# Two multiplications in GpSimd's rounding of attention weights, and one VectorE product left out

## The chip, the cores and the metric

The kernel runs on one core of one Trainium2 chip. The metric is the device time of one execution in microseconds; the median over runs is compared. The profile is taken from one execution by the hardware profiler.

## The reference

Four transformer layers follow one another on an activation x of 2 x 512 tokens by 128 features, with a context of 2 x 77 tokens. Layer 0 attends from the ten best tokens, layer 1 has single-head attention, layer 2 has 16 heads with rotary positions, and layer 3 is quantised to 8 bits. The change touches only layer 3's self-attention. Cut to what matters:

```python
def _fq(x, delta, zp, n_bits):
    xi = _round_ste(x / delta) + zp
    xq = jnp.clip(xi, 0.0, 2.0 ** n_bits - 1.0)
    return (xq - zp) * delta

# 16 heads of 8 features, 2 x 512 tokens; dq = dk = dv = 0.02, dw = 1 / 255
sim = jnp.einsum('bhid,bhjd->bhij', _fq(q, dq, 128.0, 8), _fq(k, dk, 128.0, 8)) * SCALE
attn = jax.nn.softmax(sim, axis=-1)
out = jnp.einsum('bhij,bhjd->bhid', _fq(attn, dw, 0.0, 8), _fq(v, dv, 128.0, 8))
```

So an attention weight becomes the integer nearest to exp(s - max) / (sum x dw), at most 255.

## The kernel before, in words

Each engine has its own hand-written list of instructions, and semaphores order them against each other. There is no planner: the order of each list is as it stands in the code. The self-attention of layer 3 is worked off in 64 pairs. A pair n is two heads (j = 0, 1) of one block of 128 query tokens against all 512 keys, so two tiles of 128 x 512 values. Its way through the engines:

- TensorE, `int_scores(n)` (L865): two matmuls of the integer queries and keys write the scores into two PSUM banks. Three pairs of banks take turns.
- VectorE, `maxima(n)` (L1430): the negative maximum of every row of both tiles, written to `stats[:, 0]`.
- GpSimd, `shift(n)` (L441): multiplies the two maxima of a row by the score's scale, giving `stats[:, 1]`.
- ScalarE (L1048): two activations compute exp(scale x score + shift) into one of six slots of `e_ring` and add up each row's sum in `stats[:, 3]`.
- VectorE, `recips(m)`, once for two pairs (four sums a row): L1436 multiplies the sums by the step dw (`sc(DW1)`), in place, and waits for itself; L1437 takes the reciprocal into `stats[:, 2]`.
- GpSimd, `rounded(n)` (L450), two instructions a pair: multiplies each row of 512 exponentials by its reciprocal, adds the constant 0.0 and writes int16, which rounds. The output goes to one of four slots of `t_rows`.
- The SP queue (L334): a DMA transposes the pair's 128 x 1024 integers. It waits for both roundings of the pair, and for the key conversion of the pair four before.
- VectorE, `keys(n)` (L1443): the transposed integers, cut at 255, become bf16.
- TensorE, `int_outputs(n)` (L882): the product with the integer values, accumulated in PSUM.

The orders are skewed. GpSimd's list is shift(n), then rounded(n - 3); VectorE's is maxima(n), then recips every second n (for pairs n - 3 and n - 2), then keys(n - 6); TensorE's is int_scores(n), then int_outputs(n - 7). ScalarE has one pair after the other. `rounded(n)` waits for the reciprocal of its two pairs and for the transpose of pair n - 4.

`sders` is a small tile written once by VectorE near the start of the kernel: its columns 0 to 7 are the reciprocals of the eight quantisation steps, so `sders[:, DW1]` is 1 / dw, one value on all 128 partitions. L1138, L1416 and the shift L441 read other columns of it.

On GpSimd, far ahead of this stage, two kinds of instruction alternate four times each: L385 multiplies a tile of 154 elements a row by a column and adds the constant 0.0, and L387 multiplies the same tile by a column and adds a second column. L397, in every layer norm, adds a constant to 4 elements a row.

Of the kernel before, what the change touches and what calls it, by code (L numbers as in the profile page):

```python
# [10 lines left out]
ALU = mybir.AluOpType  # L11
# [47 lines left out]
DQ1, DK1, DV1, DW1, DQ2, DK2, DV2, DW2, SCORE_B = range(9)  # L59
# [20 lines left out]
def spare_row(v):  # L80
    return BAND - 1 - DH * v
# [23 lines left out]
def build(nc, ins, out, stop=99):  # L105
    ctx = ExitStack()
    with ctx:
        def sb(name, shape, dt=F32):
            return ctx.enter_context(nc.sbuf_tensor(name, shape, dt))
# [27 lines left out]
        def S(name):  # L137
            name = shared.get(name, (name, 0))[0]
            if name not in sems:
                sems[name] = ctx.enter_context(nc.semaphore(name.replace(".", "_")))  # L140
            return sems[name]
# [58 lines left out]
        stats = sb("stats", [P, 8, 16])  # L200
        q_stack = sb("q_stack", [P, U * N], BF16)
        k_stack = sb("k_stack", [P, U * N], BF16)
        sders = sb("sders", [P, 16])
# [53 lines left out]
        def sc(k):  # L257
            return scalars[:, k:k + 1]
# [7 lines left out]
        def turned(n):  # L266

            return S(f"L3.turned{n % TURNING}"), 16 * (n // TURNING + 1)
# [76 lines left out]
        def _(pool):  # L345
# [90 lines left out]
            def shift_pairs():  # L436

                def shift(n):
                    c = 2 * (n % 8)
                    pool.wait_ge(S("ints.nm"), n + 1)  # L440
                    pool.tensor_scalar(stats[:, 1, c:c + 2], stats[:, 0, c:c + 2], sders[:, 8:9], None, ALU.mult  # L441
                                       ).then_inc(S("ints.m"), 1)

                def rounded(n):
                    pool.wait_ge(S("ints.recip"), n // 2 + 1)
                    if n >= TURNING:
                        pool.wait_ge(*turned(n - TURNING))
                    for j in range(2):
                        c = 2 * (n % 8) + j
                        pool.tensor_scalar(t_rows[n % TURNING][:, j, :], e_ring[n % len(e_ring)][:, j, :],  # L450
                                          stats[:, 2, c:c + 1], 0.0, ALU.mult, ALU.add).then_inc(S("ints.rounded"), 1)

                for n in range(PAIRS + ROUND_BEHIND):
                    if n < PAIRS:
                        shift(n)
                    if n >= ROUND_BEHIND:
                        rounded(n - ROUND_BEHIND)
# [612 lines left out]
        def _(dve):  # L1070
            own = [0]

            def then(ins):

                own[0] += 1
                ins.then_inc(S("dve.own"), 1)
                dve.wait_ge(S("dve.own"), own[0])
# [233 lines left out]
            s = ps[0:80, 7, 0:4 * M].rearrange("p (n m) -> p n m", m=M)  # L1311
# [45 lines left out]
            if stop >= 2:  # L1357
# [31 lines left out]
                for i in range(T):  # L1389
                    dve.wait_ge(S("heads.sc"), count("L2.ca", "sc") + i + 1)  # L1390
                    at = i * V * P + spare_row(0)
                    c = P + spare_row(1) - spare_row(0)
                    nm = neg_max[:, at:at + V * c].rearrange("p (v c) -> p v c", c=c)[:, :, 0:3 * BAND + 1:BAND]
                    s = ps[:, 4 * (i % 2):4 * (i % 2) + 4, 0:V * M].rearrange("p j (v m) -> p v j m", v=V)
# [8 lines left out]
            if stop >= 3:  # L1403
# [29 lines left out]
                def recips(m):  # L1433
                    s, r = (stats[:, k, 4 * (m % 4):4 * (m % 4) + 4] for k in (3, 2))
                    dve.wait_ge(S("ints.exp"), 4 * (m + 1))
                    then(dve.tensor_scalar(s, s, sc(DW1), None, ALU.mult))  # L1436
                    dve.reciprocal(r, s).then_inc(S("ints.recip"), 1)  # L1437

                def keys(n):
# [6 lines left out]
                for n in range(PAIRS + KEYS_BEHIND):  # L1446
                    if n < PAIRS:
                        maxima(n)
                    m = n - ROUND_BEHIND
                    if 0 <= m < PAIRS and m % 2 == 0:  # L1450
                        recips(m // 2)
                    if n >= KEYS_BEHIND:
                        keys(n - KEYS_BEHIND)
# [9 lines left out]
                for n in range(B * FC):  # L1463
                    k, c = divmod(n, FC)
# [32 lines left out]
```

## Time and profile before

| | us |
|---|---|
| median of 3 runs | 682.29 |
| lowest, highest run | 680.37, 683.24 |
| profiled execution | 681.98 |
| its span, first to last instruction | 680.3 |
| GpSimd busy in the span | 202.8 |
| VectorE busy in the span | 413.2 |
| stretch of the 64 pairs, roughly | 403 to 532 |

Busy time is the time in which an engine has an instruction in execution. A wait for a semaphore is not part of it, but a wait that happens inside an instruction is. The chain of waits is followed back from the last instruction, at each step to what released it or to the instruction before it on its engine. "issue" in it is time in which the engine waited for nothing that the profile shows.

### The profile page before, as it was taken

To read this page: it belongs to the slowest core of one execution; us is meant where nothing else is said; L and a number is where in the kernel's file an instruction comes from. 1 tells how busy PE (TensorE), PEld (TensorE's weight loads), DVE (VectorE), ACT (ScalarE), POOL (GpSimd) and SP (SyncE) were. 2 spreads that over 40 slices of the span, in tenths; PEclk is the share of its full clock that TensorE was granted. 3 is DMA by queue.
4 is the path that set the end of the run, shared out by engine and by line. 5 is a ranking of instruction groups with operands and counts; after the bars stand their busy time and mean duration, and the time that the engine had idled before them with its cause. 6 is when DMAs were issued, how large, how long until landed. Compare 5 with 4: busy or idle time off the path is not lost.

```text
span 680.3 us, 8234 instructions
## 1 busy us (share of the span) xinstructions
PE 443.0 (65%) x2905; PEld 243.9 (36%) x2905; DVE 413.2 (61%) x854; ACT 248.0 (36%) x481; POOL 202.8 (30%) x354
## 2 busy tenths in 40 slices
PE   6578459266767998758986635556655435545577
PEld 3445245133334333425243511222222313334435
DVE  3625470758896111258333489899998478888543
ACT  2014123021001666310624119888886112313131
POOL 3220222500000334240002209899989200000020
PEclk9559658688898999865977875555555665555569
DMA  9100000000000000000000006887887200000001
GB/s 281 50 0 1 1 0 1 0 0 1 1 1 1 1 1 1 1 1 0 1 1 0 1 0 121 133 148 139 142 142 144 27 0 0 1 0 1 0 1 31
DMA packets 75804, 23.43 MB, mean 34 GB/s; under 512 B 67894, under 2 KB 74996, under 8 KB 75764
## 3 DMA queue, kind: packets, MB, share of 16 engines
q1 hardware_dynamic: 75763, 22.91, 17.5%
q8 instruction: 23, 0.38, 0.2%
q14 instruction: 18, 0.14, 0.1%
HBM read 5.60 MB, written 0.52 MB: 9 GB/s over the span
## 4 chain that ended last, share of the span: by engine, by line
PE 38%; DVE 30%; POOL 19%; issue 8%; ACT 3%; DMA 1%; ACTq 0%; DVEq 0%; POOLq 0%
POOL k_stack L450 12%; DVE k_stack L1380 6%; PE ps L631 3%; DVE xh L1093 3%; PE ps L563 3%; POOL stats L441 3%; PE ps L486 3%; PE ps L587 3%; PE ps L671 3%; PE ps L617 3%; PE ps L556 2%; PE ps L482 2%; POOL rstd L399 2%; DVE cr_max L1186 2%; PE ps L578 2%
## 5 line engine op out<-in xcount | busy, mean ns | idle before, releaser
L397 POOL TENSOR_SCALAR rstd<-mv 128x4 f32<-128x4 f32 x18 | 4.1, 227 | 268.6 <-DVE mv L1088 268.5
L1430 DVE TENSOR_REDUCE stats<-ps 128x2 f32<-128x1024 f32 x64 | 77.4, 1213 | 1.8 <-PE ps L865 1.8
L960 ACT ACTIVATE e_buf<-ps 128x1024 f32<-128x1024 f32 (+4 forms) x56 | 39.7, 771 | 106.0 <-PE ps L617 105.3
L1048 ACT ACTIVATE e_buf<-ps,stats,sders 128x512 f32<-128x512 f32 x88 | 67.6, 775 | 25.7 <-POOL stats L441 25.6
L882 PE MATMUL ps<-k_stack,q_stack 128*32 128x128 bf16 x512 | 39.2, 308 | 46.8 <-DVE k_stack L1443 46.7
L450 POOL TENSOR_SCALAR k_stack<-e_buf,stats 128x512 int16<-128x512 f32 x88 | 62.4, 721 | 1.4
L671 PE MATMUL ps<-ident,e_buf 128*77 128x128 f32 x128 | 33.3, 430 | 34.9 <-ACT e_buf L969 34.9
L1380 DVE TENSOR_REDUCE k_stack<-ps 128x4 f32<-128x512 f32 (+3 forms) x32 | 46.1, 1488 | 9.5 <-PE ps L590 9.5
L882 PEld LDWEIGHTS ps<-k_stack,q_stack 128*32 128x32 bf16 x512 | 22.3, 129 | 77.0 <-DVE k_stack L1443 76.5
L347 POOL TENSOR_SCALAR_AFFINE_SELECT e_buf<-e_buf 128x256 f32<-128x256 f32 x44 | 17.6, 407 | 107.4 <-ACT e_buf L960 106.4
L865 PE MATMUL ps<-q_stack 32*128 32x512 bf16 x128 | 38.0, 603 | 14.0 <-DVE q_stack L1424 7.4
L482 PE MATMUL ps<-ident,xh 128*128 128x128 f32 x72 | 19.3, 432 | 41.7 <-DVE xh L1093 41.7
L587 PE MATMUL ps<-q_stack,qT 32*128 32x128 f32 (+3 forms) x256 | 29.7, 537 | 21.7 <-DVE k_stack L1380 11.7
L1107 DVE TENSOR_TENSOR x<-ps,x 128x512 f32<-128x512 f32 x14 | 9.7, 692 | 51.8 <-PE ps L563 38.1
L671 PEld LDWEIGHTS ps<-ident,e_buf 128*77 128x77 f32 x128 | 25.1, 243 | 39.9 <-ACT e_buf L969 39.9
L1443 DVE TENSOR_SCALAR k_stack<-k_stack 128x1024 bf16<-128x1024 int16 x64 | 28.8, 449 | 11.8 <-DMA k_stack<-k_stack 11.6
L919 ACT ACTIVATE xT<-ps,cols 128x512 f32<-128x512 f32 x12 | 9.3, 777 | 72.7 <-PE ps L482 72.7
L617 PE MATMUL ps<-k_stack,q_stack 32*128 32x512 f32 (+3 forms) x256 | 33.8, 477 | 0.7 <-ACT e_buf L960 0.6
L1159 DVE COPY o_sb<-ps 128x512 f32<-128x512 f32 x16 | 11.0, 687 | 36.1 <-PE ps L631 36.1
L1048 ACT ACTIVATE t_buf<-ps,stats,sders 128x512 f32<-128x512 f32 x40 | 30.8, 777 | 3.1 <-POOL stats L441 3.1
L1093 DVE TENSOR_SCALAR xh<-x,mv,rstd 128x128 f32<-128x128 f32 x72 | 28.5, 458 | 4.0 <-POOL rstd L399 4.0
L482 PEld LDWEIGHTS ps<-ident,xh 128*128 128x128 f32 x72 | 13.3, 219 | 45.7 <-DVE xh L1093 45.2
(250 smaller groups left out, 953.2 us busy)
## 6 DMA issues: line engine op xcount, KB each, us to landing
wsq<-in_squares SPq DMA_DIRECT2D x3, 384.0 KB, 5.0
k_stack<-k_stack SPq DMA_TRANSPOSE x64, 3.1
spread<-in_spread SPq DMA_DIRECT2D x1, 896.0 KB, 6.8
x<-in_x SPq DMA_DIRECT2D x1, 512.0 KB, 4.4
l_w<-in_L_xattn_W_ff SPq DMA_DIRECT2D x2, 256.0 KB, 7.2
l_w<-in_L_xattn_fc_w SPq DMA_DIRECT2D x2, 256.0 KB, 7.8
l_w<-in_L_xattn_ff_w SPq DMA_DIRECT2D x1, 512.0 KB, 8.8
out<-x SPq DMA_DIRECT2D x2, 256.0 KB, 2.3
```

What stands on the lines that cost most here:

```text
L450: pool.tensor_scalar(t_rows[n % TURNING][:, j, :], e_ring[n % len(e_ring)][:, j, :], stats[:, 2, c:c + 1], 0.0, ALU.mult, ALU.add).then_in ...
L482: mm = pe.transpose(ps[:, k, t * P:(t + 1) * P], src[:, k * QB + t, :], ident[:, :])
L587: mm = pe.matmul(ps[:, 4 * (i % 2) + j, 0:n], qT[r, at:at + P], keys(r), start=True, stop=not causal)
L617: mm = pe.matmul(ps[0:rows, 2 * slot + j % 2, 0:N - kb * P], keys(b, v, r, kb), q_shift[r, b, v, kb * P:N], start=True, stop=True)
L671: mm = pe.transpose(ps[0:M, 3 + c % 2, j * P:(j + 1) * P], e_buf[:, i % 2, h * M:(h + 1) * M], ident[:, :])
L865: mm = pe.matmul(ps[:, 2 * (n % 3) + j % 2, :], tile(q_int, b * QB + qb)[r, :], k_band[r, v, b * N:(b + 1) * N], start=True, stop=True)
L882: mm = pe.matmul(ps[BAND * band:BAND * (band + 1), 7, qb * P:(qb + 1) * P], v_band[:, kb, b, V * band + v, :], t_keys[n % len(t_keys)][:, ...
L960: act.activation(e_ring[n % len(e_ring)][0:rows, :, 0:N - kb * P], ps[0:rows, 2 * (n % 3):2 * (n % 3) + 2, 0:N - kb * P], ACT.Exp).then_in ...
L1048: act.activation(e_ring[n % len(e_ring)][:, j, :], ps[:, 2 * (n % 3) + j, :], ACT.Exp, bias=stats[:, 1, c:c + 1], scale=sders[:, 8:9], acc ...
L1093: ins = dve.tensor_scalar(xh[:, t, :], x[:, t, :], mv[:, t, 0:1], rstd[:, t:t + 1], ALU.subtract, ALU.mult)
L1380: dve.tensor_reduce(nm, ps[:, 4 * (i % 2):4 * (i % 2) + 4, 0:(qb + 1) * P], AX, ALU.max, negate=True).then_inc(S("heads.max"), 1)
L1430: dve.tensor_reduce(stats[:, 0, c:c + 2], ps[:, 2 * (n % 3):2 * (n % 3) + 2, :], AX, ALU.max, negate=True).then_inc(S("ints.nm"), 1)
```

## The change

The rounding's second scalar operand is the column 1 / dw in place of the constant 0.0, and its second operation a multiplication in place of an addition. The product of sum and dw on VectorE, with the wait for it, is left out; the reciprocal is taken of the sum itself. The integer that results is that of exp x (1 / sum) x (1 / dw).

```diff
@@ -448,7 +448,8 @@
                     for j in range(2):
                         c = 2 * (n % 8) + j
                         pool.tensor_scalar(t_rows[n % TURNING][:, j, :], e_ring[n % len(e_ring)][:, j, :],
-                                          stats[:, 2, c:c + 1], 0.0, ALU.mult, ALU.add).then_inc(S("ints.rounded"), 1)
+                                          stats[:, 2, c:c + 1], sders[:, DW1:DW1 + 1], ALU.mult, ALU.mult
+                                           ).then_inc(S("ints.rounded"), 1)
 
                 for n in range(PAIRS + ROUND_BEHIND):
                     if n < PAIRS:
@@ -1433,7 +1434,6 @@
                 def recips(m):
                     s, r = (stats[:, k, 4 * (m % 4):4 * (m % 4) + 4] for k in (3, 2))
                     dve.wait_ge(S("ints.exp"), 4 * (m + 1))
-                    then(dve.tensor_scalar(s, s, sc(DW1), None, ALU.mult))
                     dve.reciprocal(r, s).then_inc(S("ints.recip"), 1)
 
                 def keys(n):
```

## Rows read from the trace of the kernel before

**Rows 1.** The page's first part: busy us (share of the span) and instructions.
```profile
PE 443.0 (65%) x2905; PEld 243.9 (36%) x2905; DVE 413.2 (61%) x854; ACT 248.0 (36%) x481; POOL 202.8 (30%) x354
```

**Rows 2.** Windows, stretch 409 to 527 us: length, busy us by engine, clock, DMA.
```profile
409.00:527.00 118.00, 69.95 (x614) 27.42 (x614) 108.06 (x184) 99.21 (x248) 110.17 (x189) 0.50 0.80 139
```

**Rows 3.** Chain of waits, 409 to 527 us: shares by line.
```profile
by line: POOL k_stack L450 68.7%; POOL stats L441 17.8%; issue 13.5%; POOLq L447 0.1%
```

**Rows 4.** Timeline of GpSimd: start us, duration us, instruction, count.
```profile
417.48 0.53 POOL L441 TENSOR_SCALAR stats<-stats,sders 128x2 f32<-128x2 f32 x1
...
424.68 0.43 POOL L441 TENSOR_SCALAR stats<-stats,sders 128x2 f32<-128x2 f32 x1
425.08 1.35 POOL L450 TENSOR_SCALAR k_stack<-e_buf,stats 128x512 int16<-128x512 f32 x2
426.42 0.28 POOL L441 TENSOR_SCALAR stats<-stats,sders 128x2 f32<-128x2 f32 x1
426.76 1.46 POOL L450 TENSOR_SCALAR k_stack<-t_buf,stats 128x512 int16<-128x512 f32 x2
428.23 0.42 POOL L441 TENSOR_SCALAR stats<-stats,sders 128x2 f32<-128x2 f32 x1
```

**Rows 5.** Timeline of VectorE, same round.
```profile
426.01 0.45 DVE L1436 TENSOR_SCALAR stats<-stats,scalars 128x4 f32<-128x4 f32 x1
426.49 0.18 DVE L1437 RECIPROCAL stats<-stats 128x4 f32<-128x4 f32 x1
426.59 0.41 DVE L1443 TENSOR_SCALAR k_stack<-k_stack 128x1024 bf16<-128x1024 int16 x1
...
428.05 0.45 DVE L1443 TENSOR_SCALAR k_stack<-k_stack 128x1024 bf16<-128x1024 int16 x1
```

**Rows 6.** Timeline of GpSimd at the start of the stage.
```profile
410.51 0.29 POOL L441 TENSOR_SCALAR stats<-stats,sders 128x2 f32<-128x2 f32 x1
410.77 1.36 POOL L450 TENSOR_SCALAR k_stack<-e_buf,stats 128x512 int16<-128x512 f32 x2
412.10 0.29 POOL L441 TENSOR_SCALAR stats<-stats,sders 128x2 f32<-128x2 f32 x1
412.46 1.36 POOL L450 TENSOR_SCALAR k_stack<-e_buf,stats 128x512 int16<-128x512 f32 x2
```

**Rows 7.** Lines L385, L387: ns min/median/max, then three of their rows in the timeline.
```profile
L385 POOL TENSOR_SCALAR km<-kc,band_mask x4: 396/408/426, 29.4 to 32.0; 128x154 f32<-128x154 f32 x4
L387 POOL TENSOR_SCALAR k<-kc,band_mask,band_one x4: 465/484/503, 29.8 to 32.4; 128x154 f32<-128x154 f32 x4
...
29.84 0.47 POOL L387 TENSOR_SCALAR k<-kc,band_mask,band_one 128x154 f32<-128x154 f32 x1
30.29 0.40 POOL L385 TENSOR_SCALAR km<-kc,band_mask 128x154 f32<-128x154 f32 x1
30.67 0.50 POOL L387 TENSOR_SCALAR k<-kc,band_mask,band_one 128x154 f32<-128x154 f32 x1
```

**Rows 8.** Single lines over the whole kernel: ns min/median/max, first and last start.
```profile
L450 POOL TENSOR_SCALAR k_stack<-e_buf,stats x88: 685/687/964, 409.2 to 526.2; 128x512 int16<-128x512 f32 x88
L441 POOL TENSOR_SCALAR stats<-stats,sders x64: 282/290/528, 404.8 to 520.7; 128x2 f32<-128x2 f32 x64
L1436 DVE TENSOR_SCALAR stats<-stats,scalars x32: 214/452/653, 408.6 to 522.8; 128x4 f32<-128x4 f32 x32
L397 POOL TENSOR_SCALAR rstd<-mv x18: 224/228/241, 72.3 to 648.6; 128x4 f32<-128x4 f32 x18
```

**Rows 9.** Late transposes: landing times, waits of 409 to 527 us, two timeline rows.
```profile
DMA to landing us min/median/max: 3.0/3.1/5.3
...
POOL stats L441 <- DVE stats L1430: 7.2, 6, 1.8
...
435.36 0.43 DVE L1443 TENSOR_SCALAR k_stack<-k_stack 128x1024 bf16<-128x1024 int16 x1 [1.60 <-DMA k_stack<-k_stack]
437.02 0.39 POOL L441 TENSOR_SCALAR stats<-stats,sders 128x2 f32<-128x2 f32 x1 [1.80 <-DVE stats L1430]
```

## The prediction

> **What bounds the kernel now.** I read the page's busy line first and the table of windows second. Over the whole kernel no engine stands out, but in the stretch of the change, 409 to 527 us, GpSimd is busy 110.2 of 118.0 us and VectorE 108.1, with ScalarE at 99.2 and the DMA engines at 0.80 [rows 1, 2]. Two engines are nearly full, so the share alone does not say which one a saving must be made on. The chain of waits for that stretch does: 68.7% is the rounding of L450, 17.8% the shift of L441, the rest issue, and no VectorE line is in it [rows 3]. The timeline of GpSimd shows why: in one round of two pairs, 424.68 to 428.23 us, that is 3.55 us, its instructions touch each other, two roundings, a shift, two roundings, a shift, with one visible gap of 0.06 us ahead of the rounding at 426.76 [rows 4].
>
> VectorE looks as full in its own timeline, but part of that is waiting inside an instruction. The product of L1436 has 4 elements and takes 0.45 us here, from 426.01 to 426.46, and over the stage it runs from 214 to 653 ns, median 452 [rows 5, 8]. It ends as the rounding on GpSimd ends (425.08 + 1.35 = 426.43) [rows 4, 5]. So about 0.24 of its 0.45 us is VectorE standing behind GpSimd, and VectorE has that much to spare in a round.
>
> The opposite also shows. The shift takes 0.43 and 0.42 us where VectorE's key conversion L1443 runs beside it (428.05 to 428.50), and 0.28 where none does; two roundings take 1.46 beside the L1443 of 426.59, and 1.35 without [rows 4, 5]. Undisturbed spacing stands at the stage's start: two roundings 1.33 us (410.77 to 412.10), a shift 0.26 (410.51 to 410.77) [rows 6]. A round of GpSimd without collisions is thus 2 x (1.33 + 0.26) = 3.18 us; the measured 3.55 holds 0.37 more: two collisions of about 0.14 each with L1443, and 0.09 of waiting for the reciprocal.
>
> By the Trainium skill (SBUF — State Buffer, Who interferes with whom) GpSimd and a VectorE instruction in a 2-port mode hold one port pair exclusively, so that "the other fully blocks". The trace agrees in kind (0.45 against 0.214 us for L1436). What that rule alone would promise from dropping a port user is not found on GpSimd's side: the shift that follows L1436 takes its least, 0.28.
>
> **The change part by part.** The stage has 64 pairs, 128 roundings and 32 calls of recips.
>
> First, the rounding's second scalar becomes a column in place of the constant 0.0: 128 instructions, all on the chain. The kernel has the same contrast elsewhere on GpSimd. L385 multiplies 154 elements by a column and adds the constant 0.0; L387 multiplies by a column and adds a column, same size, alternating with it. Their least durations are 396 and 465 ns (69 apart), their medians 408 and 484 (76 apart), and their starts give 0.45 us from L387 to the next and 0.38 from L385 to the next (29.84, 30.29, 30.67) [rows 7]. Is this price per instruction or per element? An instruction with one column costs 0.26 us of spacing at 2 elements and 1.33 / 2 = 0.665 at 512, so 0.79 ns an element [rows 6]; that line gives 0.38 at 154 elements, which is what L385 shows. So the one-column form has a fixed part of about 0.26 us. L397, with 4 elements and no column at all, has a median of 228 ns against 290 for the shift L441 with one column [rows 8], so the first column costs about 60 ns at a size where elements cost nothing. The second, at 69, is nearest to that: I take it as fixed. 128 x 0.069 = +8.8 us. Bounds: 0 below (if the read of the second column hides behind the 512 elements), and above it grows with the elements, 0.076 x 512 / 154 = 0.25 us each, +32 us. Below nothing is excluded: the new form has no fewer operands or operations. The second operation also turns from an add into a multiplication, for which no GpSimd row exists; as both are one operation an element I take no difference, and the same +32 covers a slower multiplication.
>
> By the Trainium skill (Advanced Engine Details and Errata, GPSIMD Details) a per-partition read on GpSimd has about 50 ns of latency; by that, an estimate, the sum's term would be 128 x 0.05 = 6.4 us in place of 8.8, and the sum 684.2 us. The least durations of L385 and L387, 69 ns apart, are taken instead.
>
> Second, VectorE's L1436 goes: 32 instructions of 0.45 us and the wait behind them; from its start to that of the reciprocal it is 426.01 to 426.49 = 0.48 us [rows 5]. None of this lies on the chain except at one point: the reciprocal ends at 426.49 + 0.18 = 426.67 and the rounding that needs it starts at 426.76, 0.34 us after its shift's start, where an undisturbed one starts 0.26 after [rows 4 to 6]. With the reciprocal 0.48 earlier GpSimd never waits for it. The wait was 0.08 to 0.10 us in some 30 rounds: -2.7 us. Bounds: 0 and 32 x 0.10 = -3.2.
>
> Third, transposes that land late. Their landing takes 3.1 us, at most 5.3 [rows 9]. Where one is late, VectorE's L1443 waits (1.60 us at 435.36), its maximum L1430 of the next pair is late, and GpSimd's shift stands idle: 1.80 us at 437.02. In the stretch there are six such idle times with 7.2 us together; the first, 1.46 us, is the start of the stage, so 5.7 us are five late landings [rows 9]. L1443 of pair n - 6 needs a rounding three pairs behind the shift, so slower pairs give the landing more time: with roundings 0.14 us longer a pair and the wait and jitter taken off, about 0.1 x 3 = 0.3 us of each. 5 x 0.3 = -1.5 us. Bounds: 0, and all 5.7 us if VectorE, 0.48 us a round lighter, gets far enough ahead; it is held back by the same transposes, so I stay near the low end.
>
> Fourth, collisions. L1443 stays, 64 times, and now arrives about 0.4 us earlier in every second pair. Each costs GpSimd 0.14 us today. The dearest row is the shift of 0.53 us at 417.48, 0.25 above its least [rows 4]; the cheapest is 0.10. L1436 itself cost GpSimd nothing. I take no change: 0. Bounds: 64 x (0.25 - 0.14) = +7 us and, if they all vanish, 64 x 0.14 = -9 us.
>
> Sum: +8.8 - 2.7 - 1.5 + 0 = +4.6 us. By rounds: 3.55 + 4 x 0.069 - 0.09 = 3.74 us, 32 rounds. The profiled execution took 681.98 us for a span of 680.3, so 686.6; the median of the runs is 682.29, 0.3 above it, well inside their own scatter (680.37 to 683.24). Everything ahead of the stage and behind it is the same code; TensorE is at half its full clock through the stage (granted 0.50, the level of 1.2 GHz) [rows 2] and is not waited for, so a slower pair costs nothing there.
>
> **The rivals.**
> - VectorE is what holds the round. For: it is 108.1 of 118 us busy with hardly a gap, and its L1443 is what stretches shifts. Against: the chain has no VectorE line, and L1436 is stretched to the end of GpSimd's instruction. Place: every round; it decides if, with VectorE 0.48 us lighter, collisions disappear from GpSimd's path. Then the round falls to GpSimd's own floor, 3.18 + 4 x 0.069 = 3.46 us, 0.09 below today's, 32 x 0.09 = 2.9 us, with 1.5 of the late landings: 682.0 - 4.4 = 677.6. Faster. Chance 15%.
> - The second column is free at 512 elements. For: nothing but the larger size. Against: the column's 69 ns at 154 elements look fixed. 682.0 - 2.7 - 1.5 = 677.8. Chance 15%.
> - The collisions grow: L1443, now early, lands more often where the shift cost 0.53 us. +7 on the sum: 693.6. Chance 12%.
> - The price is by element, or the multiplication is slower than the add: +32 - 4 = 710. For: no row has the form. Against: L385 lies on the one-column line and the 69 ns match the first column's 60. Chance 5%.
> - The change doesn't do what it says: the product on VectorE is shorter than a wait that takes its place. VectorE would wait on transposes in its stead; this is in the first case, as it costs nothing there.
>
> **How the numbers follow.** The forecast has 53%, its own range 683.5 to 690 (columns at 55 to 76 ns, late landings 0 to -3). What a measurement of this kernel can tell from no change is 0.5%, 3.4 us, so 678.9 to 685.7 is the same. Slower: 40 of the forecast's 53, the 12 and the 5: 0.57. Faster: 9 of the 15 and 8 of the 15: 0.17. Same: 0.26. The range that holds 8 in 10 goes from 677.5 to 693: it leaves out most of the 5% and half of the 12% above, and some of the two faster cases below.
>
> **What would show it.** In the profile after: L450's least duration 0.75 us against 685 ns [rows 8]; no L1436 row; the reciprocal done before the shift ends, and a spacing of 0.26 to 0.28 from shift to rounding where L1443 is not beside it; a round of 3.74 us; L450 and L441 alone still in the chain; idle ahead of the shift some 1.5 us less; VectorE busy 13 us less in the stage. The forecast is wrong if L450 still takes 0.69 us, if it takes over 0.9, or if the round is 3.5 us with longer roundings, which would say that collisions went.

## The result

The changed kernel took a median of 687.72 us against 682.59 for the kernel before on the same chip: a ratio of 1.0082, 95% interval 1.0059 to 1.0105. One of its six executions took 946.87 us; the ratio leaves it out, and without it the median is 687.70. In a later comparison, the run e7 below, the ratio was 1.0097 (1.0067 to 1.0127). The forecast was 686.6 and slower. The change costs 5.1 and 5.4 us by the medians of the two comparisons, 5.6 and 6.6 us by their ratios.

### The profile page after: what moved, and what is told of

It reads as the page before. It is cut to its first block, busy times and chain, and to the rows that moved or that the text cites. A ratio compares the mean times of both kernels' runs of the same rounds, so it can differ in the third digit from the quotient of the medians.

```text
span 686.0 us, 8202 instructions
## 1 busy us (share of the span) xinstructions
PE 441.2 (64%) x2905; PEld 243.3 (35%) x2905; DVE 418.3 (61%) x822; ACT 249.2 (36%) x481; POOL 215.2 (31%) x354
## 4 chain that ended last, share of the span: by engine, by line
PE 37%; DVE 29%; POOL 19%; issue 10%; ACT 3%; DMA 1%; ACTq 0%; DVEq 0%; POOLq 0%
POOL k_stack L450 10%; DVE k_stack L1381 5%; POOL stats L441 4%; PE ps L632 3%; DVE xh L1094 3%; PE ps L564 3%; PE ps L487 3%; PE ps L588 3%; PE ps L618 3%; PE ps L672 3%; PE ps L557 2%; PE ps L483 2%; POOL rstd L399 2%; DVE cr_max L1187 2%; PE ps L579 2%
## 5 line engine op out<-in xcount | busy, mean ns | idle before, releaser
L397 POOL TENSOR_SCALAR rstd<-mv 128x4 f32<-128x4 f32 x18 | 4.1, 229 | 268.3 <-DVE mv L1089 268.2
L1431 DVE TENSOR_REDUCE stats<-ps 128x2 f32<-128x1024 f32 x64 | 77.1, 1208 | 2.3 <-PE ps L866 2.3
L450 POOL TENSOR_SCALAR k_stack<-e_buf,stats,sders 128x512 int16<-128x512 f32 x88 | 68.0, 783 | 0.0
L1443 DVE TENSOR_SCALAR k_stack<-k_stack 128x1024 bf16<-128x1024 int16 x64 | 47.7, 745 | 13.2 <-DMA k_stack<-k_stack 13.2
L441 POOL TENSOR_SCALAR stats<-stats,sders 128x2 f32<-128x2 f32 x64 | 27.4, 427 | 21.5 <-DVE stats L1431 21.5
```

The source lines that it names most:

```text
L1431: dve.tensor_reduce(stats[:, 0, c:c + 2], ps[:, 2 * (n % 3):2 * (n % 3) + 2, :], AX, ALU.max, negate=True).then_inc(S("ints.nm"), 1)
L1443: dve.tensor_scalar(t_keys[n % len(t_keys)], t_turned[n % TURNING], QMAX, None, ALU.min).then_inc(S("ints.pt"), 1)
```

## The profile after

In the changed kernel L450 and L441 keep their numbers, the maximum is L1431 (L1430 before), the reciprocal stays L1437, the key conversion L1443. First the page's busy line, then the windows of the stage, then the shares of the chain there:

```profile
PE 441.2 (64%) x2905; PEld 243.3 (35%) x2905; DVE 418.3 (61%) x822; ACT 249.2 (36%) x481; POOL 215.2 (31%) x354
```

```profile
409.00:533.00 124.00, 70.08 (x608) 27.19 (x608) 113.14 (x153) 101.10 (x250) 121.00 (x188) 0.50 0.76 131
```

```profile
by line: POOL k_stack L450 57.1%; issue 21.7%; POOL stats L441 21.3%; DVE stats L1431 1.0%; POOLq L447 0.1%
```

GpSimd is busy 12.4 us longer over the kernel [rows 1]. VectorE lost 32 instructions and is busy 5 us more over the kernel, where the prediction had it 13 us less in the stage: what the products gave back its key conversions took, and more, as the two lines of L1443 below show. The chain is GpSimd's two lines again, but not these alone: VectorE's maximum has 1.0% of it. In the stage GpSimd fills 121.0 of 124.0 us, against 110.2 of 118.0 [rows 2]. Single lines, ns min/median/max, three of the changed kernel and then L1443 of the kernel before:

```profile
L450 POOL TENSOR_SCALAR k_stack<-e_buf,stats,sders x88: 764/767/1041, 409.8 to 533.6; 128x512 int16<-128x512 f32 x88
L441 POOL TENSOR_SCALAR stats<-stats,sders x64: 284/448/542, 405.6 to 527.5; 128x2 f32<-128x2 f32 x64
L1443 DVE TENSOR_SCALAR k_stack<-k_stack x64: 387/793/1052, 414.6 to 538.7; 128x1024 bf16<-128x1024 int16 x64
...
L1443 DVE TENSOR_SCALAR k_stack<-k_stack x64: 396/427/770, 414.0 to 531.3; 128x1024 bf16<-128x1024 int16 x64
```

The rounding went from a median of 687 to 767 ns, and the shift, which nobody touched, from 290 to 448 [rows 8]. GpSimd's timeline, start and duration in us:

```profile
424.56 0.47 POOL L441 TENSOR_SCALAR stats<-stats,sders 128x2 f32<-128x2 f32 x1
425.01 1.52 POOL L450 TENSOR_SCALAR k_stack<-e_buf,stats,sders 128x512 int16<-128x512 f32 x2
426.51 0.47 POOL L441 TENSOR_SCALAR stats<-stats,sders 128x2 f32<-128x2 f32 x1
426.96 1.51 POOL L450 TENSOR_SCALAR k_stack<-e_buf,stats,sders 128x512 int16<-128x512 f32 x2
428.46 0.47 POOL L441 TENSOR_SCALAR stats<-stats,sders 128x2 f32<-128x2 f32 x1
```

And VectorE's beside it:

```profile
425.93 0.89 DVE L1443 TENSOR_SCALAR k_stack<-k_stack 128x1024 bf16<-128x1024 int16 x1
426.75 1.21 DVE L1431 TENSOR_REDUCE stats<-ps 128x2 f32<-128x1024 f32 x1
427.88 0.16 DVE L1437 RECIPROCAL stats<-stats 128x4 f32<-128x4 f32 x1
427.96 0.81 DVE L1443 TENSOR_SCALAR k_stack<-k_stack 128x1024 bf16<-128x1024 int16 x1
```

A round is now 428.46 - 424.56 = 3.90 us (3.85 later in the stage), against 3.55. Two roundings are spaced at 1.50 in place of 1.33, and both shifts of a round at 0.45 (0.43 later in the stage) in place of 0.40 and 0.34 [rows 4]. VectorE's conversion takes 0.8 to 0.9 us here in place of 0.41 and 0.45 [rows 5]: it arrives early, stands behind GpSimd's second rounding (which ends at 426.5) and runs out beside the shift, in both pairs. The idle time ahead of the shift, from the waits of 403 to 540 us:

```profile
POOL stats L441 <- DVE stats L1431: 21.5, 8, 15.9
```

19.0 of these are the four at the stage's start (15.92, 0.82, 0.83, 1.46), so 2.5 us are left to late transposes, where it was 5.7 [rows 9].

The profiled executions are 5.7 us apart (spans of 680.3 and 686.0 us), but the stage alone costs more. From its first shift to the start of its last conversion it takes 6.7 us longer (404.8 to 531.3 before, 405.6 to 538.7 after). The changed kernel enters the stage 0.7 us later, and behind it, from the next layer norm (L397, at 537.64 and 545.11) to the end, it takes 140.9 us in place of 142.7, with the same code. TensorE's granted clock is what differs there: in the last stretch, from L397 at 647.2 and at 654.4 to the end, its mean is 0.85 before and 0.89 after, between its levels of 1.2 and 2.4 GHz, and the stretch takes 33.1 and 31.6 us.

## The experiments

Ratios are to the kernel before in the same comparison.

**e1, the product kept.** Does leaving out VectorE's product do anything once the column is there?

```diff
                     dve.wait_ge(S("ints.exp"), 4 * (m + 1))
+                    then(dve.tensor_scalar(stats[:, 4, 4 * (m % 4):4 * (m % 4) + 4], s, sc(DW1), None, ALU.mult))
                     dve.reciprocal(r, s).then_inc(S("ints.recip"), 1)
```

> The changed kernel with VectorE's product of sum and step still made, with its wait, into a tile that nothing reads. GpSimd's instructions are exactly those of the changed kernel, VectorE's those of the kernel before. Theory 1 (the column costs about 0.083 us an instruction, half of the measured spacing 1.495 against 1.33 us for two roundings, and dropping the product gives back the wait for the reciprocal, 2.7 us, and some of the late transposes): the rounding stays at 0.75 us of spacing, the gap ahead of every second pair of roundings comes back, and the time is 690 to 692, so 2 to 4 us above the changed kernel. Theory 2 (dropping the product does harm, since the key conversion now falls on the shift in every pair): with the product kept the collisions are as before, 0.14 us in place of 0.17 to 0.19, and the time is 1 to 3 us below the changed kernel, 685 to 687. Theory 3 (VectorE's load matters to nothing): 687.7.

Measured: 688.62 us, ratio 1.0089 (1.0065 to 1.0112), not to be told from the changed kernel. Its timeline of GpSimd:

```profile
422.11 0.28 POOL L441 TENSOR_SCALAR stats<-stats,sders 128x2 f32<-128x2 f32 x1
422.46 1.62 POOL L450 TENSOR_SCALAR k_stack<-e_buf,stats,sders 128x512 int16<-128x512 f32 x2
424.06 0.44 POOL L441 TENSOR_SCALAR stats<-stats,sders 128x2 f32<-128x2 f32 x1
424.48 1.51 POOL L450 TENSOR_SCALAR k_stack<-e_buf,stats,sders 128x512 int16<-128x512 f32 x2
425.98 0.28 POOL L441 TENSOR_SCALAR stats<-stats,sders 128x2 f32<-128x2 f32 x1
```

A round is 425.98 - 422.11 = 3.87 us. The gap for the reciprocal is back (0.35 from shift to rounding, where 0.26 is undisturbed) and one of the two conversions falls on a rounding (1.62 against 1.51), not on a shift. The gap of 0.09 and this collision of 0.10 together cost what the second collision with a shift, 0.17 to 0.19, costs in the changed kernel. Of the three theories the third gives the time, but for a reason that it did not have: the first and the second were both at work and cancel.

**e2, the constant 255.** The change without its column.

```diff
-                                          stats[:, 2, c:c + 1], sders[:, DW1:DW1 + 1], ALU.mult, ALU.mult
+                                          stats[:, 2, c:c + 1], QMAX, ALU.mult, ALU.mult
```

> The changed kernel with the second multiplication by the constant 255.0 in the instruction in place of the column 1 / step (the same number for these inputs; what it leaves out is reading the step of the attention weights from the input). VectorE's product stays out. Theory 1 (the price is that of a second column, and none is in the multiplication): the rounding takes 685 ns again, and what is left is the reciprocal's wait and the late transposes: 682.5 - 2.7 - 1 = 679, between 677 and 681. Rival (the price is in the second multiplication against an addition): the rounding takes about 765 ns and the time is 687.7. Rival (VectorE was a second bound all along): without the column the round falls from 3.55 to 3.2 us, and the time to 671 or below.

Measured: 680.11 us, ratio 0.9961 (0.9946 to 0.9976), and the rounding at 687 ns median again.

```profile
421.89 0.45 POOL L441 TENSOR_SCALAR stats<-stats,sders 128x2 f32<-128x2 f32 x1
422.31 1.35 POOL L450 TENSOR_SCALAR k_stack<-e_buf,stats 128x512 int16<-128x512 f32 x2
423.65 0.45 POOL L441 TENSOR_SCALAR stats<-stats,sders 128x2 f32<-128x2 f32 x1
```

Here a pair takes 423.65 - 421.89 = 1.76 us and the round 3.51, with the shift spaced at 0.42 and two roundings at 1.34. The second multiplication is free; the whole price is the column's: 1.0082 / 0.9961 from the two comparisons, 1.2% or 8.3 us between kernels that differ in nothing else. VectorE's saving alone gives 0.4%. The rival with VectorE as a second bound is out: the round is 3.51, not 3.2. Both conversions of a round fall on the shift here too (0.42 of spacing each), so the gap of 0.08 to 0.09 is gone, 0.04 of it comes back as collisions, and the late landings stay at 5.7 us.

**e3, the reciprocals first.** VectorE's `recips` stands ahead of `maxima(n)` in the kernel before:

```diff
-                    if n < PAIRS:
-                        maxima(n)
                     m = n - ROUND_BEHIND
                     if 0 <= m < PAIRS and m % 2 == 0:
                         recips(m // 2)
+                    if n < PAIRS:
+                        maxima(n)
```

> The kernel before with one edit in VectorE's order: the reciprocals of two pairs stand ahead of the maximum of the pair, not behind it. The same instructions in all. It takes away the wait of GpSimd's rounding for the reciprocal and leaves VectorE's load as it was. Theory 1 (the wait of 0.08 to 0.10 us a round is on the chain): 682.5 - 2.7 = 680, and the spacing from shift to rounding is 0.26 where no key conversion is beside it. Rival (VectorE itself has no room: it now stands in front of the maximum waiting for exponentials): the maximum comes late, GpSimd waits for it ahead of the shift, and the time is 683 to 690.

Measured: 684.85 us, ratio 1.0046 (1.003 to 1.0062): the rival. GpSimd now waits ahead of the shift once a round:

```profile
424.94 0.40 POOL L441 TENSOR_SCALAR stats<-stats,sders 128x2 f32<-128x2 f32 x1 [0.25 <-DVE stats L1430]
```

The gap ahead of the rounding is gone, and 0.25 us ahead of the shift stand in its place; the round is 3.74 us. Both conversions now fall on shifts (0.40 and 0.45 us of duration). The same product cannot be made earlier at no cost.

**m1 and m2, GpSimd's forms.** m1 had all forms on one source line, and the profile merges such rows; m2 repeats it with a line for each. Behind the kernel before, after its last use of the tiles (m2, shortened to the sizes of 512):

```diff
+            for at in range(...):
+                pool.tensor_scalar(k_int16[:, at:at + 512], xT[:, 0:512], c0, 0.0, ALU.mult, ALU.add)   # L500
+            ...                                                        c0, c1, ALU.mult, ALU.mult       # L502
+            ...                                                        c0, c1, ALU.mult, ALU.add        # L504
+            ...                                                        c0, 1.0, ALU.mult, ALU.mult      # L506
+            ...                                                        c0, None, ALU.mult               # L508
+            ...                                                        1.0, 0.0, ALU.mult, ALU.add      # L510
```

> The kernel before, and behind its last use of the tiles, on GpSimd alone with nothing beside it, four instructions in a row of each of six forms at 2, 154 and 512 elements a row and of the first four at 1024: column and constant (multiply, add), two columns (multiply, multiply), two columns (multiply, add), column and constant (multiply, multiply), column alone, two constants (multiply, add). All from float32 to int16. Its time means nothing; the spacing of the starts does. Theory 1: the second column adds 0.07 to 0.09 us at every size, multiply and add cost the same, and the first column costs some 0.06 over none. Rival (the price is by the element): 0.07 at 154 elements, 0.25 at 512, 0.5 at 1024. Rival (the price is in the multiplication): column and constant with two multiplications costs as much as two columns.

> The same measurement of GpSimd's forms as in m1_forms, with a source line for each form and size, so that each can be read by itself. Behind the kernel before, nothing beside it. Its time means nothing. Theory 1: the second column adds 0.07 to 0.09 us at 2, 154, 512 and 1024 elements alike; a second multiplication by a constant costs what the addition costs. Rival by the element: 0.25 us at 512 and 0.5 at 1024. Rival by the operation: two multiplications with a constant cost as much as two columns.

m2's timeline of GpSimd, four instructions to a row; the spacing of one is a quarter of the step from one start to the next:

```profile
694.52 2.70 POOL L500 TENSOR_SCALAR k_stack<-xT,sders 128x512 int16<-128x512 f32 x4
697.20 3.01 POOL L502 TENSOR_SCALAR k_stack<-xT,sders 128x512 int16<-128x512 f32 x4
700.19 3.01 POOL L504 TENSOR_SCALAR k_stack<-xT,sders 128x512 int16<-128x512 f32 x4
703.18 2.69 POOL L506 TENSOR_SCALAR k_stack<-xT,sders 128x512 int16<-128x512 f32 x4
705.84 6.19 POOL L508 TENSOR_SCALAR k_stack<-xT,sders 128x512 int16<-128x512 f32 x4
712.00 2.37 POOL L510 TENSOR_SCALAR k_stack<-xT 128x512 int16<-128x512 f32 x4
714.35 4.41 POOL L512 TENSOR_SCALAR q_stack<-xT,sders 128x1024 int16<-128x1024 f32 x4
718.74 4.71 POOL L514 TENSOR_SCALAR q_stack<-xT,sders 128x1024 int16<-128x1024 f32 x4
723.43 4.72 POOL L516 TENSOR_SCALAR q_stack<-xT,sders 128x1024 int16<-128x1024 f32 x4
```

At 512 elements: column and constant 0.67 us, two columns 0.75 with either operation, column and constant with two multiplications 0.67, no column 0.59. At 1024: 1.10 and 1.17. At 2 and 154 elements the same steps gave 0.24 and 0.32, 0.38 and 0.46. The second column costs 0.073 to 0.078 us at every size, by the instruction and not by the element. A first column costs 0.08 over none. The column with no second operation was not expected: 1.54 us. The shift L441 is of this form, which at 2 elements costs 0.26 against 0.24.

**e4, half of the key conversion**, on the changed kernel:

```diff
-                    dve.tensor_scalar(t_keys[n % len(t_keys)], t_turned[n % TURNING], QMAX, None, ALU.min
+                    w = 2 * N if n < len(t_keys) else N
+                    dve.tensor_scalar(t_keys[n % len(t_keys)][:, 0:w], t_turned[n % TURNING][:, 0:w], QMAX, None, ALU.min
```

> The changed kernel with VectorE's key conversion cut to the first half of its 1024 columns, from the fourth pair on (it leaves out the cut at 255 and the conversion of the second head's weights, which keep stale values). It halves the time for which the conversion and GpSimd can be in each other's way, and touches no instruction of GpSimd. Theory 1 (in the changed kernel every conversion waits for the end of a rounding and then holds up the shift behind it, 0.17 us each, by its own length): the shift falls from 0.45 to about 0.30 to 0.33 us, 64 x 0.13 = 8 us, and the time is 679 to 682. Rival (the shift is longer for another reason, such as the VectorE reduction or the matmuls that run beside it): the shift stays at 0.45 and the time at 687. Rival (the transposes hold the pace): the shift falls, but GpSimd then waits ahead of it, and the time falls by less than 3 us.

Measured: 681.11 us, ratio 0.9988 (0.9967 to 1.001), against 1.0082 for the changed kernel: 0.9%, 6.4 us, for work that GpSimd does not do.

```profile
423.68 0.33 POOL L441 TENSOR_SCALAR stats<-stats,sders 128x2 f32<-128x2 f32 x1
423.99 1.51 POOL L450 TENSOR_SCALAR k_stack<-e_buf,stats,sders 128x512 int16<-128x512 f32 x2
425.49 0.33 POOL L441 TENSOR_SCALAR stats<-stats,sders 128x2 f32<-128x2 f32 x1
```

The shift is 0.33 us where it was 0.47, its spacing 0.31. The collision is real, and a conversion of half the length costs GpSimd 0.05 in place of 0.17 to 0.19. That the total fell less than 8 us fits the idle time ahead of the shift, 23.8 us after 21.5.

**e5, the product in PSUM**, on the kernel before:

```diff
-                    then(dve.tensor_scalar(s, s, sc(DW1), None, ALU.mult))
-                    dve.reciprocal(r, s).then_inc(S("ints.recip"), 1)
+                    steps = ps[:, 6, 4 * (m % 4):4 * (m % 4) + 4]
+                    then(dve.tensor_scalar(steps, s, sc(DW1), None, ALU.mult))
+                    dve.reciprocal(r, steps).then_inc(S("ints.recip"), 1)
```

> The kernel before with VectorE's product of sum and step written to a free PSUM bank, where the reciprocal reads it, in place of writing it back to the statistics tile. GpSimd keeps its one column and its constant. Theory 1 (the 0.24 us by which the product is stretched are VectorE standing behind GpSimd's rounding for the SBUF ports, which an output in PSUM does not use, and the reciprocal's wait follows from that): the product takes some 0.2 us, the reciprocal is done before the shift ends, and the time comes to that of the kernel with the constant 255, 679 to 681, with the step still read from the input. Rival (the product is stretched by its input in SBUF, or for another reason): it still takes 0.45 us and the time is that of the kernel before, 682. Rival (reading or writing PSUM costs as much as was saved): product and reciprocal together as long as before, 682 to 684.

Measured: 681.67 us, ratio 0.9992 (0.9976 to 1.0008). First the product's line, ns min/median/max:

```profile
L1437 DVE TENSOR_SCALAR ps<-stats,scalars x32: 207/209/225, 407.2 to 522.3; 128x4 f32<-128x4 f32 x32
```

The stretch is gone, 209 ns against a median of 452 [rows 8], so the product no longer stands behind GpSimd, as the first theory had it. In e1, where its output goes to another column in SBUF, it takes 612 ns at the median, so writing in place is not the reason. Whether it is SBUF's ports, as the theory says, no trace shows; the run shows that the output's place decides. The time was not as the theory had it:

```profile
425.39 0.50 POOL L441 TENSOR_SCALAR stats<-stats,sders 128x2 f32<-128x2 f32 x1
425.87 1.35 POOL L450 TENSOR_SCALAR k_stack<-t_buf,stats 128x512 int16<-128x512 f32 x2
427.20 0.45 POOL L441 TENSOR_SCALAR stats<-stats,sders 128x2 f32<-128x2 f32 x1
427.62 1.35 POOL L450 TENSOR_SCALAR k_stack<-t_buf,stats 128x512 int16<-128x512 f32 x2
428.96 0.50 POOL L441 TENSOR_SCALAR stats<-stats,sders 128x2 f32<-128x2 f32 x1
```

The gap for the reciprocal is gone, but both conversions fall on shifts (0.48 and 0.42 of spacing), and the round is 3.57 us. What VectorE gives back, its conversions take.

**e6 and e8, no conversion.** If the collisions are what stands in the way, a kernel without L1443 should show it. GpSimd's free constant makes room: with 1024.0 added and float16 output the weights come out as whole numbers that TensorE can take as they are. Both kernels also have e5's product in PSUM, eight slots for transposed tiles, float16 values and 128 small matmuls ahead of the stage that sum the values, so they are not one-edit experiments. Cut, against the kernel before:

```diff
+TURNED = 8
+OFFSET = 1024.0
...
-                                          stats[:, 2, c:c + 1], 0.0, ALU.mult, ALU.add).then_inc(S("ints.rounded"), 1)
+                                          stats[:, 2, c:c + 1], OFFSET, ALU.mult, ALU.add).then_inc(S("ints.rounded"), 1)
...
-                    if n >= KEYS_BEHIND:
-                        keys(n - KEYS_BEHIND)
...
-                    pe.wait_ge(S("ints.pt"), n + 1)
+                    pe.wait_ge(*turned(n))
...
-                    act.activation(half(xT, b), ps[:, 7, :], ACT.Identity, scale=sders[:, 10:11]).then_inc(S("state.T"), 1)
+                    act.activation(half(xT, b), ps[:, 7, :], ACT.Identity, scale=sders[:, 10:11],
+                                   bias=value_sum[:, b:b + 1]).then_inc(S("state.T"), 1)
```

> A version built on what the earlier runs showed: the constant 0.0 of GpSimd's rounding costs nothing and is free for use, and each key conversion on VectorE costs GpSimd 0.12 to 0.22 us. GpSimd multiplies by the reciprocal column, adds the constant 1024.0 and writes float16, whose values from 1024 to 2048 are whole numbers; the transposed tile goes to TensorE as it is, and VectorE's conversion is left out (with it the cut at 255, which no weight exceeds at this step). The 1024 is taken out again by a bias in ScalarE's copy of the outputs, from the sums of the values. Eight slots for transposed tiles in place of four; VectorE's product goes to PSUM as in the run before. Theory 1 (the round is GpSimd's: undisturbed 2 x (1.33 + 0.26) = 3.18 us against 3.55, and late transposes no longer hold up VectorE's maximum): 682 - 32 x 0.37 - 4 = 666, between 663 and 671; the shift takes 0.28 and the rounding 0.69 everywhere. Rival (ScalarE is the next bound, with two activations of 1.51 us a pair, and it or the transposes catch the pace): the round stays above 3.3 us and the time above 672. Rival (float16 output is slower on GpSimd than int16): the rounding takes over 0.75 us and the gain is gone.

Measured: 685.66 us, ratio 1.0085 (1.0067 to 1.0103). The slow round and the lost gain are in the rivals' forecasts, but the roundings are not longer, only further apart, and none of the three theories names that:

```profile
423.39 1.48 POOL L453 TENSOR_SCALAR k_stack<-e_buf,stats 128x512 f16<-128x512 f32 x2
424.95 0.29 POOL L444 TENSOR_SCALAR stats<-stats,sders 128x2 f32<-128x2 f32 x1
425.33 1.47 POOL L453 TENSOR_SCALAR k_stack<-e_buf,stats 128x512 f16<-128x512 f32 x2
426.90 0.29 POOL L444 TENSOR_SCALAR stats<-stats,sders 128x2 f32<-128x2 f32 x1
```

The shift is back at 0.29, the collisions are gone, and a rounding takes 692 ns against 687. But two roundings are spaced at 1.56 us and the shift at 0.38: some 0.1 us lies between any two instructions, in no duration. The next two runs look for it, with GpSimd alone.

```diff
+                ins = pool.tensor_scalar(..., xT[:, 0:512], c0, CONSTANT, ALU.mult, ALU.add)   # shortened: one line for each output type and constant
```

> GpSimd alone again, behind the kernel before, at 512 elements a row, four instructions in a row of each: multiply by a column and add a constant (0.0, 1024.0) to int16, to float16 and to bfloat16, the column alone to bfloat16, int16 and float32, and column and 0.0 to float32. Its time means nothing. It asks where the 0.1 us between the instructions of the kernel without the conversion comes from, and why the column alone took 1565 ns at 512 elements. Theory: the output type sets it (int16 spaced at 0.665 us, float16 at 0.78 with a duration of 0.69), the constant's value has no part, and the form without a second operation takes about 1.56 us whatever the output. Rival: the constant 1024.0 costs it, so int16 with 1024.0 is spaced at 0.78 too. Rival: neither, and all are spaced at 0.67, so that the gaps come from what ran beside GpSimd.

```profile
679.35 2.99 POOL L478 TENSOR_SCALAR k_stack<-xT,sders 128x512 int16<-128x512 f32 x4
682.41 2.69 POOL L480 TENSOR_SCALAR k_stack<-xT,sders 128x512 f16<-128x512 f32 x4
685.18 2.99 POOL L482 TENSOR_SCALAR k_stack<-xT,sders 128x512 f16<-128x512 f32 x4
688.25 2.69 POOL L484 TENSOR_SCALAR k_stack<-xT,sders 128x512 bf16<-128x512 f32 x4
```

L478 and L482 add 1024.0 to int16 and float16, L480 and L484 add 0.0. The four of a row take 2.99 with the one constant and 2.69 with the other, whatever the output: 0.1 us for each of three gaps. The rival with the constant is right. The column alone was spaced at 1.54 to 1.55 us to every output type.

> GpSimd alone behind the kernel before, 512 elements a row, float32 to int16: a column multiplied, and one of fourteen constants added (0, 1, 255, 512, 1023, 1024, 1025, 1100.7, 1280, 1536, 1791, 2048, -1024, 1024 again), four instructions each; then 1024 as the second multiplication. Its time means nothing. The run before had 0.0 spaced at 0.67 us and 1024.0 at 0.77, with the same duration. Theory: the spacing hangs on the constant in a way that leaves a free one between 1024 and 1792, with which the kernel without the conversion would lose its 0.1 us an instruction and come to 666 to 672 us. Rival: every added constant but 0.0 costs 0.1 us, then adding is dearer than multiplying by 255 or 1 was, and no such offset is free.

```profile
689.14 2.72 POOL L484 TENSOR_SCALAR k_stack<-xT,sders 128x512 int16<-128x512 f32 x4
691.93 3.00 POOL L486 TENSOR_SCALAR k_stack<-xT,sders 128x512 int16<-128x512 f32 x4
```

L484 adds 1023, L486 1024. 0, 1, 255, 512 and 1023 took 2.70 to 2.72 us for four; the ten rows with 1024, 1025, 1100.7, 1280, 1536, 1791, 2048, -1024, 1024 again and 1024 as a factor took 3.00. They come in this order, but in m3, where 0.0 and 1024.0 take turns, it is the constant and not the place that decides. No offset of e6's kind is free, but one of 512 in half steps is:

```diff
-OFFSET = 1024.0
+OFFSET = 512.0
...
-                    then(dve.tensor_scalar(steps, s, sc(DW1), None, ALU.mult))
+                    then(dve.tensor_scalar(steps, s, sc(DW1), 2.0, ALU.mult, ALU.mult))
...
+                then(dve.tensor_scalar(twice[:, :], sders[:, 10:11], 2.0, None, ALU.mult))
```

> The kernel without the conversion, with an offset of 512.0 in place of 1024.0. In float16 the numbers from 512 to 1024 lie 0.5 apart, so the reciprocal is halved (VectorE's product takes a second factor 2.0 in the same instruction) and ScalarE's copy of the outputs has twice the scale. The cut at 255 is left out as before. No instruction is added in the loop. Theory 1 (constants of 1024 and more space GpSimd's instructions 0.1 us further apart, those up to 1023 do not): the rounding is spaced at 0.67 us, the shift at 0.26 to 0.30, the round falls from 3.9 to 3.2 to 3.3 us, and the time is 664 to 671. Rival (the gaps came from what waits on GpSimd's semaphores in that kernel, not from the constant): the spacing stays at 0.78 and the time at 685. Rival (ScalarE or the transposes are next): the rounding is spaced at 0.67, but GpSimd waits ahead of the shift, the round is 3.4 to 3.6 us and the time 672 to 680.

Measured: 672.27 us, ratio 0.9833 (0.9797 to 0.9869): faster than the kernel before, and so than the changed kernel with its 1.0082.

```profile
424.35 0.31 POOL L445 TENSOR_SCALAR stats<-stats,sders 128x2 f32<-128x2 f32 x1
424.61 1.38 POOL L454 TENSOR_SCALAR k_stack<-e_buf,stats 128x512 f16<-128x512 f32 x2
425.94 0.31 POOL L445 TENSOR_SCALAR stats<-stats,sders 128x2 f32<-128x2 f32 x1
```

The round is 2 x (425.94 - 424.35) = 3.18 us, the undisturbed one that [rows 6] gave. The round is as theory 1 had it, while the time is 1 us over its range and at the low edge of the third theory's. The waits that follow show why: of the 25.2 us of idle time ahead of the shift, 21.0 are the four at the stage's start (19.0 in the kernel before), and 4.2 stay in later rounds (5.7 before), in which VectorE's maximum is late. TensorE now waits on the transposes itself.

```profile
PE ps L886 <- DMA k_stack<-k_stack: 32.4, 44, 2.3
POOL stats L445 <- DVE stats L1451: 25.2, 9, 16.6
```

**e7, the changed kernel again.**

```diff
(the changed kernel, no edit)
```

> The changed kernel itself, once more, against the kernel before on the same chip. The two theories differ on what dropping VectorE's product is worth with the column in place: theory 1 had 2 to 4 us, the kernel with the product kept came out at a ratio of 1.0089 (1.0065 to 1.0112) and the changed kernel at 1.0082 (1.0059 to 1.0105). If the product is worth 3 us the ratio here is 1.0045 or below; if it is worth nothing beside the collisions that take its place, it is 1.0075 to 1.0095 again.

Measured: 686.52 us, ratio 1.0097 (1.0067 to 1.0127). Against 1.0089 for e1, with the column in place the product is worth nothing that can be measured; the intervals leave room for some 2 us either way.

## Why the prediction was right

The direction was right, and so was the step that carries the change, the price of a second column. The round was not: 3.74 us forecast, 3.85 to 3.90 measured. That the time came within 1.1 us of 686.6 is in part luck, as the terms show.

- **What bounds the stage.** GpSimd's instructions, as predicted. e2 settles it: VectorE 0.48 us a round lighter, GpSimd's spacing for two roundings still 1.34 against 1.33, and the round falls by 0.04 us.
- **The second column, +8.8 us.** Right in kind and in form, by the instruction, a little small. Two roundings went from 1.33 to 1.50 us of spacing: 0.083 each, 128 x 0.083 = +10.6. GpSimd alone has 0.078 at 512 elements; where the other 0.005 comes from was not tried. Of the two differences between L385 and L387 the smaller, 69 ns, was taken; the medians' 76 was nearer. The measured price is also outside the 55 to 76 ns of the forecast's own range. The working behind it mixed two forms: the 0.26 us at 2 elements are a shift's, which has no second operation, and the 0.665 at 512 a rounding's, which has one. m2 shows that the two forms part by 0.87 us at 512 elements and by only 0.02 at 2, so the line held because the mix was made at the small end. The first column, taken as 60 ns from L397 and L441, is 0.08 us in m2.
- **The product and its wait, -2.7 us.** The gap for the reciprocal did go. The prediction's step fails where it counted this as a gain by itself.
- **Collisions, 0.** This is the term that was missed. In the changed kernel both conversions of a round fall on the shift, at 0.17 to 0.19 us, where before one fell on the shift and one on a rounding, at some 0.14 each. A round holds 3.18 + 4 x 0.083 = 3.51 undisturbed (3.52 is measured at the stage's start) and 3.85 to 3.90 measured, so 0.34 to 0.39 of collisions against 0.28: +2 to +3.5 us. It eats the gain of the step before. This is part of the way to the rival in which collisions grow, which had +7. e2, e1, e5 and e3 show the same exchange in other ways, and e4 that a shorter conversion costs less.
- **Late transposes, -1.5 us.** 2.5 - 5.7 = -3.2 us: more than taken, inside the bounds. The reason given, that slower pairs give a landing more time, fits: with VectorE's product gone but rounds of 3.51 (e2) the idle time stays 5.7, and with the product kept but rounds of 3.87 (e1) it is 3.3. One execution of each was traced, and e5 has 7.1 at rounds of 3.57, so part of this is scatter.
- **Sum.** 10.6 - 2.7 + 2.7 - 3.2 = +7.4 us, where the forecast had +4.6: the error at the late transposes (-1.7) hid part of the other two (+1.8 and +2.7). The traces have +6.7 for the stage and +5.7 for the whole execution, the runs +5.1 by the medians. What brought the whole nearer to +4.6 than the stage was no term of the prediction: the 1.8 us that the changed kernel's profiled execution takes less behind the stage, where TensorE's granted clock was higher. That this clock comes from the change is not shown: it differs between executions of one kernel too (0.702 to 0.711 as a mean over the whole, in 23 runs of the kernel before).

By the Trainium skill (GPSIMD Engine Reference, Performance pitfalls for Q7 kernels) a small read command costs about 102 cycles that do not overlap with the one before, some 85 ns at the page's clock, an estimate. The 73 to 83 ns measured for a second column are nearer to that than to the 50 ns of the rule weighed in the prediction, but no run here shows that a column is read by such a command. By the Trainium skill (SBUF — State Buffer, Who interferes with whom) which of the two blocks the other is a matter of issue order. e3 agrees: with the same instructions in another order, both conversions fall on shifts (0.40 and 0.45 us against 0.29), where in the kernel before one of two fell on a rounding.

## What to carry to other kernels

Where two engines hold each other up, taking work off the one that waits need not shorten the round: in the changed kernel and in e5 its next instruction arrived earlier and collided elsewhere. What shortened the round was less of the work that collides (e4, e8). Price an operand that is read per partition by the instruction, and look for a row in which two like forms stand side by side, as L385 and L387 did. A constant operand that does nothing is a free place for work, as long as the constant is a cheap one: e8 used it to drop a whole instruction of the other engine. And a forecast that comes out right is still to be checked term by term: here errors of different signs and a stretch that nobody had changed made up the difference.

## What the runs showed of the hardware

- GpSimd, 512 float32 elements: a column multiplied and nothing more takes 1.54 us, with 0.0 added 0.67 (m2). Leaving an operation out makes the instruction 2.3 times as long, to int16, bfloat16 and float32 alike (m3); at 2 elements 0.26 against 0.24.
- GpSimd: a second column costs 0.073 to 0.078 us an instruction at 2, 154, 512 and 1024 elements (m2).
- GpSimd: with a constant of 1024 or more in size, the instructions lie 0.1 us further apart, at the same duration in m3 (692 and 693 ns); up to 1023 they do not (m3, m4). Thirteen constants fall on their side of that line; why, no run here shows.
- VectorE's small product in SBUF takes 452 ns at the median in the kernel before, where it arrives during a rounding and ends with it, 612 in e1, where it arrives earlier in the rounding, and 232 in e3, where it comes after a conversion. With its output in PSUM it takes 209 ns, though it still arrives during a rounding (e5).
- A key conversion of 128 x 1024 values on VectorE makes the GpSimd instruction beside it 0.10 to 0.22 us longer (e1, e5), one of half the size 0.05 (e4), and without it the shift stays at 0.29 (e6).
